# Layer norm of a four-layer graph network: minus the mean kept for the third layer only, and the epsilon of the second layer added by GpSimd

## The reference

```python
def _layernorm(x, axis=-1, eps=1e-05):
    m = jnp.mean(x, axis=axis, keepdims=True)
    v = jnp.var(x, axis=axis, keepdims=True)
    return (x - m) / jnp.sqrt(v + eps)

h = jnp.maximum(_layernorm(x, axis=-1), 0.0)
x = x + _L0_gnn_ref(h, adj, L0_gnn_Wq, L0_gnn_Wk, L0_gnn_Wv)
h = jnp.maximum(_layernorm(x, axis=-1), 0.0)
x = x + _L1_gnn_ref(h, L1_gnn_W, L1_gnn_a, L1_gnn_beta, adj)
h = jnp.maximum(_layernorm(x, axis=-1), 0.0)
x = x + _L2_gnn_ref(h, adj, L2_gnn_weight, L2_gnn_bias)
h = jnp.maximum(_layernorm(x, axis=-1), 0.0)
x = x + _L3_gnn_ref(h, adj, L3_gnn_Wq, ..., L3_gnn_bo)
```

## Time and profile before

| | us |
|---|---|
| median of 3 runs | 774.73 |
| lowest and highest | 774.39 to 776.27 |
| the profiled execution | 775.35 |
| its span in the profile | 773.6 |
| outside the span | 1.75 |

### The profile page before, as it was taken

One profiled execution on the slowest core, in us unless ns is written; L12 is line 12 of the kernel. 1 busy time (PEld: TensorE's weight loads), 2 busy tenths in 40 slices (PEclk: granted clock), 3 DMA queues, 4 the chain that ended last, 5 costly groups with the idle time before them and its releaser, 6 DMA issues.

```text
span 773.6 us, 23203 instructions
## 1 busy us (share of the span) xinstructions
PE 720.5 (93%) x7001; PEld 667.8 (86%) x7001; DVE 646.1 (84%) x2709; ACT 552.5 (71%) x1768; POOL 486.3 (63%) x615
## 2 busy tenths in 40 slices
PE   3999999999799999969999899999999999999995
PEld 3899999999577777759999799999999999999994
DVE  4688888887699999978998888888888888888873
ACT  2445455454377787855774699999999999999995
POOL 1254555545577778757886676666676666676653
PEclk9899999999899999988999999999999999999999
DMA  6223300000000000000000000000000000000001
GB/s 200 89 90 95 91 18 0 0 0 0 2 0 2 1 1 2 2 0 1 0 0 0 3 25 18 28 28 28 28 27 14 28 28 28 28 27 14 28 28 42
DMA packets 21662, 20.10 MB, mean 26 GB/s; under 512 B 2416, under 2 KB 21616, under 8 KB 21616
## 3 DMA queue, kind: packets, MB, share of 16 engines
q1 hardware_dynamic: 19440, 18.16, 7.5%
q10 hardware_dynamic: 2176, 1.44, 0.6%
HBM read 11.21 MB, written 8.39 MB: 25 GB/s over the span
## 4 chain that ended last, share of the span: by engine, by line
PE 75%; DVE 17%; issue 3%; POOL 1%; ACT 1%; DVEq 0%; POOLq 0%; ACTq 0%
PE bank L374 41%; PE bank L1058 7%; PE bank L1050 5%; PE bank L1068 4%; PE bank L152 4%; PE bank L426 4%; PE bank L439 3%; PE bank L354 3%; DVE stats L115 3%; DVE xs L829 2%; DVE masked_e L805 2%; DVE leaky_e L810 2%; DVE small L813 2%; PE bank L364 1%; DVE att L823 1%
## 5 line engine op out<-in xcount | busy, mean ns | idle before, releaser
L1127 ACT ACTIVATE prob<-wide,small 128x128 f32<-128x128 f32 x512 | 199.0, 395 | 20.1 <-DVE small L1211 20.1
L1176 POOL TENSOR_TENSOR prob<-prob,small 128x512 f32<-128x512 f32 x128 | 133.3, 1041 | 104.7 <-DVE small L1225 104.7
L141 POOL TENSOR_TENSOR rstd<-vare,mhalf 128x2 f32<-128x2 f32 x128 | 88.8, 693 | 74.2 <-DVE vare L130 74.2
L1211 DVE CUSTOM_DVE_ANT_0 wide<-bank,mbias 128x128 f32<-128x128 f32 x512 | 116.0, 283 | 9.4 <-PE bank L1050 9.4
L115 DVE BATCH_NORM_STATS2 stats<-xs 128x6 f32<-128x256 f32 (+1 forms) x256 | 95.4, 415 | 5.6 <-DMA xs<-in_x_dram 4.5
L1127 ACT ACTIVATION_READ_ACCUMULATOR prob<-wide,small 128x1 f32 x512 | 98.3, 192 | 0.0
L345 POOL TENSOR_SCALAR xn<-xs,nmean,rstd 128x256 f32<-128x256 f32 x126 | 69.0, 557 | 13.7 <-POOL rstd L141 10.8
L1134 ACT COPY probT<-bank 128x512 f32<-128x512 f32 x128 | 72.0, 588 | 6.4 <-PE bank L1058 5.4
L1058 PE MATMUL bank<-ident,prob 128*128 128x128 f32 x512 | 73.8, 276 | 1.9 <-POOL prob L1176 1.9
L364 PE MATMUL bank<-w,hT 128*128 128x258 f32 x256 | 63.2, 390 | 2.2 <-DVE xs L599 1.9
L1058 PEld LDWEIGHTS bank<-ident,prob 128*128 128x128 f32 x512 | 57.0, 140 | 8.9 <-issue 6.0
(11 more groups left out here) (131 smaller groups left out, 1838.7 us busy)
## 6 DMA issues: line engine op xcount, KB each, us to landing
out_dram<-xs SPq DMA_DIRECT2D x32, 256.0 KB, 2.2
xs<-in_x_dram SPq DMA_DIRECT2D x28, 256.0 KB, 2.7
xs<-in_x_dram ACTq DMA_DIRECT2D x1, 768.0 KB, 7.5
xs<-in_x_dram ACTq DMA_DIRECT2D x1, 256.0 KB, 3.7
wq<-in_L_gnn_Wq_dram SPq DMA_DIRECT2D x1, 256.0 KB, 3.4
wk<-in_L_gnn_Wk_dram SPq DMA_DIRECT2D x1, 256.0 KB, 5.7
wv<-in_L_gnn_Wv_dram SPq DMA_DIRECT2D x1, 256.0 KB, 7.5
w<-in_L_gnn_W_dram SPq DMA_DIRECT2D x1, 256.0 KB, 8.2
```

Source lines behind the costliest of these rows:

```text
L141: nc.gpsimd.tensor_tensor(rstd[:, b, :], vare[:, b, :], mhalf[:, :], ALU.pow).then_inc(rstd_ready, 1)
L1127: ins = nc.scalar.activation(prob[:, r, i, :], wide[:, r, i, :], ACT.Exp, bias=nmax[r][:, i:i + 1], scale=-1.0, accum_out=rsum[r][:, i:i + 1])
L1176: nc.gpsimd.tensor_tensor(prob[:, r, :, :], prob[:, r, :, :], rinv[r].unsqueeze(2).to_broadcast([128, QUAD, N]), ALU.mult).then_inc(prob_r ...
L1211: nc.vector.tensor_tensor_reduce(out=wide[:, r, i, :], in0=SS[r][:, i * N:(i + 1) * N], in1=mbias[:, :], scale=-1.0, scalar=3e38, op0=ALU. ...
```

## The change

- `root_argument` gets a switch, `negate`. Only with it is `nmean` written. The third layer's calls set it; the first and fourth layer's don't.
- `centre` on GpSimd reads the mean in `mv` and subtracts it, where it added `nmean`.
- In the second layer VectorE no longer runs `root_argument`. GpSimd has a new instruction instead, `guarded_variance`, which waits for `mv` on VectorE's step semaphore, adds the epsilon and writes `vare`; `inverse_root` then waits for it as it waited for VectorE.

```diff
-        def root_argument(dve, p, dve_step, stats_ready, b=0):
+        def root_argument(dve, p, dve_step, stats_ready, b=0, negate=False):
 
             dve.wait_ge(dve_step, 2 * p + 2)
             mean, var = mv[:, b, :, 0], mv[:, b, :, 1]
-            nc.vector.scalar_tensor_tensor(nmean[:, b, :], mean, -2.0, mean, ALU.mult, ALU.add)
+            if negate:
+                nc.vector.scalar_tensor_tensor(nmean[:, b, :], mean, -2.0, mean, ALU.mult, ALU.add)
             nc.vector.scalar_tensor_tensor(vare[:, b, :], var, EPS, var, ALU.add, ALU.max).then_inc(stats_ready, 1)
...
+        def guarded_variance(pool, p, b):
+            pool.wait_ge(l1_step, 2 * p + 2)
+            nc.gpsimd.tensor_scalar(vare[:, b, :], mv[:, b, :, 1], EPS, None, ALU.add).then_inc(l1_stats_ready, 1)
+
         def centre(pool, p, b, rstd_ready, xn_ready):
             pool.wait_ge(rstd_ready, p + 1)
             for g in range(2):
-                ins = nc.gpsimd.tensor_scalar(xnb[b][:, g, :], xs[:, 2 * p + g, :], nmean[:, b, g:g + 1],
-                                              rstd[:, b, g:g + 1], ALU.add, ALU.mult)
+                ins = nc.gpsimd.tensor_scalar(xnb[b][:, g, :], xs[:, 2 * p + g, :], mv[:, b, g, 0:1],
+                                              rstd[:, b, g:g + 1], ALU.subtract, ALU.mult)
             ins.then_inc(xn_ready, 1)
...
                     if n > 0:
+                        guarded_variance(pool, n - 1, (n - 1) % 2)
                         inverse_root(pool, n - 1, l1_stats_ready, l1_rstd_ready, (n - 1) % 2)
...
                     if n < 2:
-                        layer_norm_stats(dve, n, l1_step, l1_stats_ready, n % 2)
+                        moments(dve, n, l1_step, n % 2)
+                        mean_variance(dve, n, l1_step, n % 2)
...
                     if p + 2 < PAIRS:
+                        guarded_variance(pool, p + 2, p % 2)
                         inverse_root(pool, p + 2, stats_ready, rstd_ready, p % 2)
...
-                    root_argument(dve, ahead, step_sem, ready_sem, (p + 1) % 2)
+                    if p + 3 >= PAIRS:
+                        root_argument(dve, ahead, step_sem, ready_sem, (p + 1) % 2, negate=True)
```

More of the change, by code:

```diff
@@ L123, in mean_variance, with layer_norm_stats @@
             ins.then_inc(dve_step, 1)
-        def root_argument(dve, p, dve_step, stats_ready, b=0):
+        def root_argument(dve, p, dve_step, stats_ready, b=0, negate=False):
             dve.wait_ge(dve_step, 2 * p + 2)
             mean, var = mv[:, b, :, 0], mv[:, b, :, 1]
-            nc.vector.scalar_tensor_tensor(nmean[:, b, :], mean, -2.0, mean, ALU.mult, ALU.add)
+            if negate:
+                nc.vector.scalar_tensor_tensor(nmean[:, b, :], mean, -2.0, mean, ALU.mult, ALU.add)
             nc.vector.scalar_tensor_tensor(vare[:, b, :], var, EPS, var, ALU.add, ALU.max).then_inc(stats_ready, 1)
-        def layer_norm_stats(dve, p, dve_step, stats_ready, b=0):
+        def layer_norm_stats(dve, p, dve_step, stats_ready, b=0, negate=False):
             moments(dve, p, dve_step, b)
             mean_variance(dve, p, dve_step, b)
-            root_argument(dve, p, dve_step, stats_ready, b)
+            root_argument(dve, p, dve_step, stats_ready, b, negate)
         def inverse_root(pool, p, stats_ready, rstd_ready, b=0):
@@ L632, in _ @@
                     if n < 2:
-                        layer_norm_stats(dve, n, l1_step, l1_stats_ready, n % 2)
+                        moments(dve, n, l1_step, n % 2)
+                        mean_variance(dve, n, l1_step, n % 2)
                     update(p - 1)
                 dve.wait_ge(l1_xn_ready, 1)
-                layer_norm_stats(dve, 2, l1_step, l1_stats_ready)
+                moments(dve, 2, l1_step)
+                mean_variance(dve, 2, l1_step)
                 copy_norm2(PAIRS - 1)
@@ L860, in _ @@
                 dve.wait_ge(l2_xn_ready, 2)
-                layer_norm_stats(dve, 3, l2_step, l2_stats_ready, 1)
+                layer_norm_stats(dve, 3, l2_step, l2_stats_ready, 1, negate=True)
                 elu(PAIRS - 3)
@@ L967, in step @@
                     if norms:
-                        root_argument(dve, p + 3, dstep, stats_ready, 1 - b)
+                        root_argument(dve, p + 3, dstep, stats_ready, 1 - b, negate=True)
                 dve.wait_ge(l1_x_done, PAIRS)
```

## The result

| | us |
|---|---|
| changed kernel, median of 4 runs | 798.10 |
| lowest and highest | 797.23 to 798.82 |
| kernel before, median of 4 runs beside them | 775.02 |
| ratio, 95% interval | 1.0293 [1.0276, 1.0309] |
| the profiled execution, and its span | 797.23, 795.1 |

The changed kernel is 23 us slower, where no change was forecast and 777.2 was the upper end of the range. Most of it, 18.4 us, comes from a single word of the diff, `ALU.subtract`: in GpSimd's `centre` the instruction with the subtraction takes 2.2 times as long as the one with the addition that it replaces. The epsilon's move costs 3.8 us by itself.

What follows compares the result with a forecast made beforehand. TensorE was taken to bound the kernel except in the second layer, where VectorE is full. Terms -0.16 - 0.08 + 0.07 + 0.2 gave 0.0 us, so 774.7 us, range 770.6 to 777.2.

Steps and rivals of the forecast that it cites:

- The first and fourth layer cost nothing: First and fourth layer: nmean's slot of 0.08 us goes under TensorE's cover, vare inherits its wait; both layers at zero.
- Only the second layer matters: Only in the second layer, about 24 steps of 4.04 us where VectorE is full, can the change pay.
- The addition: GpSimd's new 128x2 adding of the epsilon, at 32 pairs: 0.19 us taken from the shift's row.
- The shift d of the loop: Second layer: change in the way from bn_aggr to the power over GpSimd, +0.01 us a step, 24 steps +0.2 us.
- the first rival: Second layer: L810 runs before centre's second half, which waits; step 3.90 us, 771.3 us in all; chance 0.30.
- L810 is held and takes back what VectorE saves: Second layer: L810 comes 0.25 us earlier inside centre's second half, is held, reads some 0.68 us; 774.7; chance 0.53 (or no effect).
- L810 slips in from d = 0.13 on: Second layer: with d above 0.13 us, L810 comes before centre's second half and runs at once; 771.3 us, chance 0.30.
- GpSimd's own time is no bound: Second layer: GpSimd idles 0.67 us a step and gets only 0.27 us more work.
- Slower: the way over GpSimd is longer: Second layer: with d = 0.10 each step is 4.14 us, +2.4 us, 777.1 in all; chance 0.13.
- The power holds L823: 798: Second layer: GpSimd's power delays attention pair L823 about 0.5 us, so L810 falls behind add; some 23 us; chance 0.02.

Runs made afterwards that it cites:

- e1: Kernel before, with GpSimd adding the epsilon in the second layer, VectorE still writing nmean and centre adding it: 779.52 us against 775.68, ratio 1.006.
- g1: Kernel before, with minus the mean of the second layer made by GpSimd, the epsilon left on VectorE: 780.03 us against 775.86, ratio 1.0045.
- f1: Changed kernel, with GpSimd making nmean after the power and centre adding instead of subtracting: 778.99 us against 775.86 for the kernel before, ratio 1.0047.
- h2: Kernel before without nmean and vare in the second layer, plus GpSimd's add waiting for the leaky rectifier L810: 772.11 us against 774.97, ratio 0.9958.
- h1: Kernel before without nmean and vare in the second layer, the power taken of the bare variance: 779.30 us against 775.86, ratio 1.004.
- i1_gate: Kernel before, with only a wait added: GpSimd's add waits for the leaky rectifier L810: 776.69 us against 774.97, ratio 1.0013.
- i2_act: Kernel before, with add waiting for L810 and ScalarE making minus the mean in the second layer: 772.50 us against 774.97, ratio 0.9958.

## Why the prediction was wrong

The part of the prediction that costs the change has a paragraph for what is removed and one for the added addition. For the swap in `centre` it has none. The swap from adding `nmean` to subtracting the mean was taken as free without a sentence, and so without a bound: the range holds nothing for it, and no rival has it. That is the step that failed. It measured +0.67 us for each of 126 instructions, +0.69 us for each step of the second layer, 18.4 us on the whole. The trace of before holds no `tensor_scalar` with a subtraction on GpSimd. For the added addition, which that trace doesn't hold either, the prediction took bounds on both sides from the nearest rows; here it took none. The nearest rows, GpSimd's `tensor_tensor` with a subtraction and with a product (0.735 and 0.667 us, below), would have said some 0.07 us an instruction, so the size itself could only come from a run.

Point by point:

- *The first and fourth layer cost nothing.* Right for taking `nmean` out. `vare` took over its wait there within 4 ns: a median of 436 in the first layer and 548 in the fourth, where `nmean` had 436 and 552:

```profile
L131 DVE SCALAR_TENSOR_TENSOR vare<-mv x29: 160/436/444, 27.8 to 179.6; 128x2 f32<-128x2 f32 x29
L131 DVE SCALAR_TENSOR_TENSOR vare<-mv x31: 160/548/985, 446.3 to 753.5; 128x2 f32<-128x2 f32 x31
```

- *Only the second layer matters.* Right, with the other sign, but for 1.34 us at the handover from the first.
- *The addition: 0.19 us, bounds 0.10 and 0.29.* It takes 0.262, within the bounds and above the value taken (0.217 in e1).
- *The shift d of the loop: +0.01, bounds -0.08 and +0.21.* Mis-sized: e1 shows +0.17. Some 0.03 of it is the addition; the power starts at 271.40, 0.39 behind the `bn_aggr`'s end and not 0.35, and then takes 0.12 more, with the attention pair now ahead of it. That the pair could be in its way stood in the first rival, but only as a help for L810 to slip in, not as a length of its own.
- *L810 is held and takes back what VectorE saves.* Right in e1 (0.67 us, forecast 0.6 to 0.7) and in g1. In the changed kernel itself it isn't seen: L819 takes 0.48 there, as the subtracting `centre` hardly holds it, and it is the attention pair that is held, by `add`.
- *L810 slips in from d = 0.13 on.* No run tests it. The 0.13 was worked out for a VectorE that is 0.25 us earlier. In e1 and g1 it is only 0.07 earlier: the leaky rectifier comes 2.07 us behind the `bn_aggr`'s end, before 2.14, and `centre`'s second half starts 1.91 to 1.93 behind it, before 1.76. By the same sum it would take a d of 0.31 there, and at 0.17 it was held, as the sum has it. In f1 it goes first, but ahead of the first half, as GpSimd is late from its own work. The step of 3.90 us that this rival gave is the one of h2, by which limit isn't shown.
- *GpSimd's own time is no bound.* This rested on 0.67 us of idle time against 0.27 of new work, and was right for those. With the two halves of `centre` at 1.35 us more GpSimd's rows add up to 4.69 us of a step of 4.89 (0.27 + 0.72 + 2.44 + 1.26), and it was the bound.
- *Slower: the way over GpSimd is longer.* 777.1 for d = 0.10, up to 0.13. e1, the nearest run to this case (VectorE keeps `nmean` there), gave 779.5 with d = 0.17: the way named was right, and d lay past the window.
- *The power holds L823: 798.* The number is the one measured, the reason is not. L832 is held by `add` and not by the power: it starts 0.03 us behind it and is free 0.17 us before its end. The agreement is chance.

## What to carry to other kernels

An edit that changes only an operation's name is an edit to be priced: look for a row with that operation, on that engine, in that form of instruction, and where there is none, bound it. Where instructions of two engines keep each other out, as the leaky rectifier and `add` do here, shortening one side moves where they meet, and a step of less work can be a slower one (h1); a wait that fixes the order can be worth more than the work saved (h2), though where the order is right already in nearly all steps it bought nothing (i1_gate). Before something is put on a second engine, count that engine's chain with the gaps between its dependent instructions, and prefer one that isn't in the loop (i2_act).

## What the runs showed of the hardware

- GpSimd's `tensor_scalar` of 128x256 fp32 takes 1.223 to 1.227 us (medians) with a subtraction in either place and 0.554 to 0.555 with addition and multiplication. Its `tensor_tensor` doesn't behave so: in the changed kernel's first layer the subtraction of the same shape takes 0.735, and the product 0.667, though the forms aren't quite the same, as the subtraction's output is fp32r:

```profile
L530 POOL TENSOR_TENSOR relsq<-relm x32: 614/667/732, 28.7 to 193.5; 128x256 f32<-128x256 f32 x32
L534 POOL TENSOR_TENSOR rels<-relm,rels x32: 727/735/745, 29.3 to 194.7; 128x256 fp32r<-128x256 f32 x32
```

- The adding `centre` holds a leaky rectifier that comes inside it (0.67 us in e1 and g1 for 0.43); the subtracting one, twice as long, doesn't: one that comes 0.89 us before the end of a half takes 0.48.
- The power of 128x2 (0.69 us) doesn't hold the attention instruction that comes 0.03 us behind it: 0.35 us, in the kernel before.
- A VectorE instruction that falls just behind `add` pays 1.04 to 1.06 us of `add`'s 1.27 (h1, changed kernel), GpSimd behind a VectorE instruction 0.16 to 0.24.
- A 128x2 `tensor_scalar` on GpSimd takes 0.22 to 0.26 us, and one that depends on it starts 0.08 to 0.2 us after it.
